# Batch 0's key maxima inside the convolution, and the last batch's first attention inside batch 0's key tile loop

## The reference, cut to what matters

```python
# layer 0: dynamic 31 tap mixing, 31 tap convolution 128 -> 512, selu, 512 -> 128
w = softmax(x @ Wl.T + bl);  y = sum_k w[..., k] * x[t + k]
z = selu(conv1d(y, Wc) + bc);  h = z @ W2.T + b2
# layer 0: causal self attention on layernorm(h), added to h, then a normalised copy added
h = h + softmax(mask(q k^T / 8)) v @ W_out + b_out;  h = h + layernorm(h)
# layer 1: cross attention of layernorm(h) on 7200 keys and values per batch
o = softmax((q w^T)(k w^T)^T / sqrt(128)) (v w^T) @ fc.T + residual;  then layernorm
# layer 1: 64 experts, top 6 of them, and shared experts
```

## Time and profile before

| | us |
|---|---|
| three runs: median (lowest to highest) | 1650.11 (1646.83 to 1660.38) |
| the profiled execution | 1647.7 |
| its span, first to last instruction | 1645.9 |
| PE busy | 1529.1 (93%) |
| DVE busy | 1052.4 (64%) |
| ACT busy | 721.6 (44%) |
| POOL busy | 559.5 (34%) |

### The profile page before, as it was taken

One profiled execution on the slowest core, in us unless ns is written; L12 is line 12 of the kernel. 1 busy time (PEld: TensorE's weight loads), 2 busy tenths in 40 slices (PEclk: granted clock), 3 DMA queues, 4 the chain that ended last, 5 costly groups with the idle time before them and its releaser, 6 DMA issues. The chain is left out here.

```text
span 1645.9 us, 30649 instructions
## 1 busy us (share of the span) xinstructions
PE 1529.1 (93%) x11598; PEld 1018.1 (62%) x11598; DVE 1052.4 (64%) x2087; ACT 721.6 (44%) x1269; POOL 559.5 (34%) x603
## 2 busy tenths in 40 slices
PE   2889998998997789999998999899999999999998
PEld 2556765765665447777777777678885444444444
DVE  4755545545234887776867777765565876877766
ACT  2231222222122126555554555456665665465554
POOL 2110001001004834602370235100795654555555
PEclk9999999999999879999999999999999999999999
DMA  8320100100001733602240223100122443344443
GB/s 218 89 89 23 29 26 17 29 26 21 1 1 53 184 88 78 143 1 73 59 123 21 65 72 94 37 23 2 54 85 88 131 130 92 123 136 132 138 130 107
DMA packets 142651, 124.74 MB, mean 76 GB/s; under 512 B 86613, under 2 KB 123949, under 8 KB 141485
## 3 DMA queue, kind: packets, MB, share of 16 engines
q1 hardware_dynamic: 127053, 110.62, 24.8%
q0 software_dynamic: 1152, 8.39, 1.6%
q10 hardware_dynamic: 14304, 3.81, 1.2%
HBM read 102.54 MB, written 5.28 MB: 66 GB/s over the span
## 5 line engine op out<-in xcount | busy, mean ns | idle before, releaser
L1186 DVE TENSOR_REDUCE region_c<-ps 120x1 f32<-120x512 f32 x336 | 225.6, 688 | 110.3 <-PE ps L1607 107.0
L873 ACT ACTIVATE region_c<-ps 128x720 f16<-128x720 f32 (+1 forms) x228 | 175.3, 769 | 274.5 <-PE ps L1637 274.5
L745 POOL TENSOR_TENSOR region_k<-region_c,region_k 128x480 f16<-128x480 f32 x198 | 217.1, 1100 | 174.0 <-ACT region_k L960 173.9
L1179 DVE TENSOR_TENSOR region_c<-ps,region_c 128x720 f16<-128x720 f32 (+1 forms) x228 | 206.1, 904 | 90.4 <-ACT ps L874 86.5
L1507 PE MATMUL ps<-region_k 128*128 128x360 f16 (+1 forms) x752 | 240.6, 320 | 5.2 <-ACT m L852 5.2
L1509 PE MATMUL ps<-region_k 128*128 128x360 f16 (+1 forms) x752 | 240.0, 319 | 0.0
L1508 PE MATMUL ps<-region_k 128*128 128x360 f16 (+1 forms) x752 | 239.7, 319 | 0.0
L665 POOL TENSOR_TENSOR vare<-mv,eps 120x6 f32<-120x6 f32 x20 | 4.0, 198 | 631.3 <-DVE mv L1111 631.3
L1654 PE MATMUL ps<-region_k,region_c 128*120 128x129 f16 (+1 forms) x1368 | 179.9, 221 | 0.0
L1655 PE MATMUL ps<-region_k,region_c 128*120 128x128 f16 (+1 forms) x1368 | 179.2, 220 | 0.0
L874 ACT ACTIVATE ps<-ps 128x720 f32<-128x720 f32 (+1 forms) x228 | 174.5, 766 | 0.0
(11 more groups left out here) (232 smaller groups left out, 2730.6 us busy)
## 6 DMA issues: line engine op xcount, KB each, us to landing
gates<-gates_dram SPq DMA_DIRECT2D x384, 120.0 KB, 2.8
region_c<-in_k SPq DMA_DIRECT2D x56, 256.0 KB, 2.7
region_c<-in_v SPq DMA_DIRECT2D x56, 256.0 KB, 2.9
region_c<-in_WcT POOLq DMA_DIRECT2D x8, 1024.0 KB, 6.4
region_c<-in_experts SPq DMA_DIRECT2D x18, 352.0 KB, 2.9
gates<-band_dram SPq DMA_DIRECT2D x26, 189.0 KB
region_k<-region_c SPq DMA_TRANSPOSE x120, 2.8
region_c<-in_xw SPq DMA_DIRECT2D x26, 63.0 KB
```

Source lines behind the costliest of these rows:

```text
L745: g.tensor_tensor(a_lo[u], ac[u], a_hi[u], ALU.subtract).then_inc(s["a_lo_ready"], 1)
L873: a.activation(halves(p_hi[u][0:parts]), st, ACT.Exp).then_inc(s["p_hi_ready"], 1)
L1179: v.tensor_tensor(halves(p_lo[u][0:parts]), two(2 * u, parts), halves(p_hi[u][0:parts]), ALU.subtract).then_inc(s["lo_ready"], 1)
L1186: v.tensor_reduce(mxk[:, r, bass.ds(c + 1, 1)], bank(bk, P), AX, ALU.max).then_inc(s["mx_free"], 1)
```

## The change

DVE's standalone list of batch 0's maxima (`prepare_tail(0)` to `shifts(0)`) goes as PE's does.

- Maxima of batch 0 become side steps of the convolution: 42 in batch 2 (quarters 6 to 47), 43 in batch 3 (quarters 0 to 42), each first in its quarter, in bank 3 with turns of `shared_turns`. Their keys come from a buffer `k16` (float16, one chunk), which GpSimd copies from `kf[0]`, whose load it issues itself (`stage_keys`); copies and variance powers are in one list on GpSimd. The maxima go to `mx0`, and `shifts(0)`, at quarter 44 of batch 3, writes `shift0`.
- The last batch's attention (`solo`) becomes steps beside batch 0's tiles 0 to 44, in bank 5 alone; on PE a step is one group: x 3 transposes, query one product of 360 columns, value 3 products of 128, score (and early) up to 480 columns, turn (and front) k + 1 transposes, weigh k + 1 products; scores of 5 and 6 blocks come in two parts (early, score; front, turn).  The end of that attention moves to tiles 45 to 56 and to tiles 0 to 14 of loop 1.
- Keys of batch 0 are split in its own loop, chunk by chunk in turn with batch 1's (`ITEMS`): chunks 0 and 1 of batch 0 before the convolution's end, then batch 1's n and batch 0's n + 2. SP's and GpSimd's lists follow it, without dynamic loops. PE waits per four tiles for batch 0's keys and turned values.
- After the convolution PE runs the first key scores, the down projections of the last batch, and goes on with the loop.

```diff
+def max_steps(b):
+    if b not in (B - 2, B - 1):
+        return []
+    if b == B - 2:
+        return [(6 + n, n) for n in range(R * NCH // 2)]
+    return [(n - R * NCH // 2, n) for n in range(R * NCH // 2, R * NCH + 1)]
...
+    steps += [(at, (MAX, 0, "max", n)) for at, n in max_steps(b)]
+    if b == B - 1:
+        steps.append((steps[-1][0] + 2, (MAX, 0, "shift", 0)))
...
-            if what not in ("logits", "band", "apply", "h"):
+            if what not in ("logits", "band", "apply", "h", "max"):
...
+END_STEPS = [("dve", "sum", 0, 0, 45), ("dve", "sum", 1, 0, 46), ("dve", "stats", 0, 0, 47), ("dve", "stats", 1, 0, 48),
+             ("dve", "stats", 2, 0, 49), ("act", "norm", 0, 0, 51), ("act", "norm", 1, 0, 52), ("dve", "add", 0, 0, 53),
+             ("dve", "add", 1, 0, 54), ("dve", "stats", 3, 0, 55), ("dve", "stats", 4, 0, 56),
+             ("dve", "stats", 5, 1, 0), ("act", "norm", 2, 1, 4), ("act", "norm", 3, 1, 5), ("pe", "x", 0, 1, 7),
+             ("act", "x", 0, 1, 8), ("pe", "x", 1, 1, 8), ("act", "x", 1, 1, 9), ("pe", "query", 0, 1, 9),
+             ("act", "query", 0, 1, 10), ("dve", "query", 0, 1, 11), ("pe", "query", 1, 1, 12),
+             ("act", "query", 1, 1, 13), ("dve", "query", 1, 1, 14)]
+SOLO_STEPS = ([("dve", "stats", 0, 0), ("dve", "stats", 1, 1), ("dve", "stats", 2, 1), ("act", "norm", 0, 4),
+               ("act", "norm", 1, 5)]
+              + [x for n, what in enumerate(("x", "query", "value")) for k in range(2)
+                 for x in (("pe", what, k, 5 + 2 * n + k), ("act", what, k, 6 + 2 * n + k))])
+for row, at in ((0, 11), (1, 16), (2, 21), (3, 26)):
+    SOLO_STEPS += [("pe", "score", row, at), ("dve", "score", row, at + 1), ("act", "score", row, at + 2),
+                   ("pe", "turn", row, at + 2), ("act", "turn", row, at + 3), ("pe", "weigh", row, at + 3),
+                   ("dve", "weigh", row, at + 4)]
+for row, at in ((4, 31), (5, 38)):
+    SOLO_STEPS += [("pe", "early", row, at), ("act", "early", row, at + 1), ("pe", "score", row, at + 1),
+                   ("dve", "score", row, at + 2), ("act", "score", row, at + 3), ("pe", "front", row, at + 3),
+                   ("act", "front", row, at + 4), ("pe", "turn", row, at + 4), ("act", "turn", row, at + 5),
+                   ("pe", "weigh", row, at + 5), ("dve", "weigh", row, at + 6)]
+SOLO, END, POST = "solo", "end", "post"
...
+ITEMS = [(0, "tail"), (0, 0), (0, 1), (1, "tail")]
+for n in range(NCH - 2):
+    ITEMS += [(1, n), (0, n + 2)]
+ITEMS += [(1, NCH - 2), (1, NCH - 1)] + [(b, c) for b in range(2, B) for c in ["tail"] + list(range(NCH))]
+DONE = {x: n + 1 for n, x in enumerate(ITEMS)}
+TURN = {x: n for n, x in enumerate(x for x in ITEMS if x[1] != "tail")}
...
+        k16 = region_c.take(CH, dtype=F16)
...
+            turns = list(TURN)
+            def turn_of(n):
+                b, c = turns[n]
+                if n == 0:
+                    sp.wait_ge(s["prod_full"], 3 * MC * B - 1)
+                if (b, c) == (1, 0):
+                    sp.wait_ge(s["shared_full"], len(SHARED))
+                turn(b, c)
+                if c == 0:
+                    turn_tail(b)
...
+                n = TURN[b, c]
+                u, at = n % 2, slice(c * CH, (c + 1) * CH)
+                if n >= 2:
+                    sp.wait_ge(s["klo_ready"], 2 + DONE[turns[n - 2]])
+                elif n == 0:
+                    sp.wait_ge(s["k16_ready"], NCH)
+                else:
+                    sp.wait_ge(s["shared_full"], SHARED[MAX, 0, "max", R * NCH][0])
+                sp.dma_start(kf[u], d["k"][b, :, at]).then_inc(s_kf[u], 16)
+                if n >= 2:
+                    sp.wait_ge(s["v_split"], DONE[turns[n - 2]])
+                sp.dma_start(vf[u], d["v"][b, :, at]).then_inc(s_vf[u], 16)
+                if n >= 2:
+                    turn_of(n - 2)
...
+            def stage_keys(c):
+                src, n = (kf[0], CH) if c < NCH else (kf_tail, TAIL)
+                if c < NCH:
+                    pool.wait_ge(s["k16_in"], 16 * (c + 1))
+                else:
+                    pool.wait_ge(s_tail, 32)
+                if c:
+                    pool.wait_ge(s["shared_full"], SHARED[MAX, 0, "max", R * c - 1][0])
+                g.tensor_copy(k16[:, 0:n], src).then_inc(s["k16_ready"], 1)
+                pool.wait_ge(s["k16_ready"], c + 1)
+                if c + 1 < NCH:
+                    pool.dma_start(kf[0], d["k"][0, :, (c + 1) * CH:(c + 2) * CH]).then_inc(s["k16_in"], 16)
+            pool.wait_ge(s["wprod_ps"], 1)
+            pool.dma_start(kf[0], d["k"][0, :, 0:CH]).then_inc(s["k16_in"], 16)
+            for b in range(1, B):
+                work = [(at + 0.25, "power", 3 * (b - 1) + x[3] + 1) for at, x in side_steps(b) if x[2] == "stats"]
+                work += [(at - 0.5, "keys", n // R) for at, n in max_steps(b) if n % R == 0]
+                for _, what, n in sorted(work):
+                    if what == "power":
+                        power_of_variance(n)
+                    else:
+                        stage_keys(n)
...
+            for b, c in ITEMS:
...
+            def first_maximum(n):
+                turn, bk = shared(0, "max", n, MAX)
+                dve.wait_ge(s["shared_full"], turn)
+                if n < R * NCH:
+                    own.link(v.tensor_reduce(mx0[:, n % R, n // R + 1:n // R + 2], bank(bk, P), AX, ALU.max))
+                else:
+                    own.link(v.tensor_reduce(mx0[:, :, 0], bank(bk, P)[:, 0:R * TAIL].rearrange("p (r k) -> p r k", r=R),
+                                             AX, ALU.max))
+                dve.sem_inc(s["dve_read"], 1)
...
+            def first_maximum(n):
+                if n == 0:
+                    pe.wait_ge(s["q_done"], 1)
+                pe.wait_ge(s["k16_ready"], n // R + 1)
+                _, bk, left, _ = SHARED[MAX, 0, "max", n]
+                pe.wait_ge(s[left[0]], left[1])
+                if n < R * NCH:
+                    last = mm(bank(bk, P), q_hi[:, 0, n % R * P:(n % R + 1) * P], k16, start=True, stop=True)
+                else:
+                    for r in range(R):
+                        last = mm(bank(bk, P)[:, r * TAIL:(r + 1) * TAIL], q_hi[:, 0, r * P:(r + 1) * P],
+                                  k16[:, 0:TAIL], start=True, stop=True)
+                last.then_inc(s["shared_full"], 1)
...
+            def solo(b, what, k):
+                x = h[:, b * R:(b + 1) * R, :]
+                if what == "stats":
+                    statistics(x, 3 * b + 1, (k,))
+                elif what == "score":
+                    dve.wait_ge(s["post_full"], USE[SOLO, b, what, k])
+                    n1 = (k + 1 if k < 4 else k - 2) * P
+                    diag = bank(5, P)[:, n1 - P:n1]
+                    own.link(v.tensor_tensor(diag, diag, causal[:], ALU.add))
+                    last = v.tensor_reduce(mx2[:, 0:1], bank(5, P)[:, 0:n1], AX, ALU.max)
+                    if k >= 4:
+                        dve.wait_ge(s["post_free"], USE[SOLO, b, "early", k])
+                        last = v.tensor_reduce(mx2[:, 1:2], pr_l[:, 0:HALF], AX, ALU.max)
+                    own.link(last)
+                    own.link(v.tensor_reduce(nm[:, k:k + 1], mx2[:, 0:1 + k // 4], AX, ALU.max, negate=True))
+                    dve.sem_inc(s["nmax_ready"], 1)
+                else:
+                    dve.wait_ge(s["post_full"], USE[SOLO, b, what, k])
+                    own.link(v.tensor_reduce(den[:, k:k + 1], sums[:, k, 0:1 + k // 4], AX, ALU.add))
+                    own.link(v.reciprocal(rden[:, k:k + 1], den[:, k:k + 1]))
+                    own.link(v.scalar_tensor_tensor(out=x[:, k, :], in0=bank(5, P)[:, 0:C], scalar=rden[:, k:k + 1],
+                                                    in1=x[:, k, :], op0=ALU.mult, op1=ALU.add))
+                    dve.sem_inc(s["post_free"], 1)
...
+                if b == 0 and t % 4 == 0:
+                    pe.wait_ge(s["klo_ready"], 2 + DONE[b, t // 4 if t < KT else "tail"])
+                at = slice(t * KW, t * KW + parts)
...
-            prepare_tail(0)
-            for k in range(2):
-                down(B - 1, k)
-            for c in range(NCH):
-                for u in range(2):
-                    for r in range(3 * u, 3 * u + 3):
-                        maximum_of(0, c // 2, c % 2, r)
-                    for what, k in LAST_ATTN_STEPS[2 * c + u:2 * c + u + 1]:
-                        attn(B - 1, what, k)
-            pe.wait_ge(s["mx_free"], MAXIMA + 1)
             pe.wait_ge(s["q_done"], B - 1)
             for b in range(B):
-                pe.wait_ge(s["klo_ready"], 2 + CHUNKS * (b + 1))
-                for u in range(2):
-                    pe.wait_ge(s_vt[u], 32 * (NCH // 2) * (b + 1))
-                pe.wait_ge(s_vt_tail, 32 * (b + 1))
-                pe.wait_ge(s["ones_columns"], b + 1 if b < 2 else 2)
+                if b:
```

(56 more changed lines are left out.)

238 lines of the change are left out of this document (132 added, 106 removed).

## The result

The changed kernel takes 1691.84 us (median of four runs, 1686.4 to 1695.31) against 1649.53 for the kernel before (four runs, 1646.83 to 1660.38). The ratio is 1.0247, 95% interval 1.022 to 1.0274. 1673 was forecast with a range of 1628 to 1694; the forecast's own range ended at 1690. The profiled execution of the changed kernel took 1686.4 us, the fastest of its four; its span is 1684.6, that of before was 1645.9. These 38.7 us are divided up here (the medians differ by 42.3).

A forecast was written before the change was run, and what follows sets the result against it. In-order TensorE, busy 95 to 99% in convolution batches 2 and 3 and the tile loops, was taken as the bound. 1647.7 - 78 (stage) + 84 (convolution) + 17 + 3 (loops) = 1673.7, say 1673 us; range 1628 to 1694.

The forecast's parts named there:

- The stage removed: Between convolution and tile loop: batch 0's maxima stage goes, saving 76.2 us, and about 2 more from starting at full clock.
- TensorE time of the maxima: Convolution batches 2 and 3: the maxima's 512 columns take 0.21 us each on TensorE, 18 us.
- (a): Convolution: band, apply or h steps wait until VectorE has reduced the maximum in bank 3; 25 us, from 10 to 32.
- (b): Convolution, ends of products 1 and 2: maxima wait behind VectorE's eviction and selu; 13 us, from 6 to 18.
- (c): Convolution: maxima wait for GpSimd's key copies queued behind variance powers, two gaps of 7.1 us included; 27 us, from 12 to 32.
- old waits: Convolution: today's TensorE waits belong to the same chains and are covered by the new ones; -7 us.
- (d): Convolution: gaps without matmuls bring three half clock spells; 8 us, from 3 to 20.
- Loop 0: Batch 0's tile loop: the attention adds TensorE work and waits for low parts; +17 us, from +12 to +24.
- the fourth rival: Loop 0: GpSimd paces it at 5.7 us a chunk, costing 5 us or so, 1678 us; chance 0.03.
- the other two that rested on overlap: Convolution: bank 3 waits overlap, not add; 1630 us (chance 0.20), or with half that overlap 1650, no change (0.20).
- Loop 1: Batch 1's tile loop: the end of the attention in its first 15 tiles; +3 us, from +2 to +8.
- The third rival: Convolution: the clock stays low through most of batches 2 and 3, 8 spells not three; +20, 1693 us; chance 0.12.

The follow-up runs named there:

- The last experiment: The version with quarter 36, with GpSimd also waiting for the convolution's last selu before splitting batch 1's key tail: 1646.62 us, lowest of versions that compute everything.
- the second kind of maxima: Changed kernel with 16 batch 2 maxima left out whose quarters have no band or apply step: 1688.48 us, ratio 1.0223.
- The experiment with GpSimd's order: Changed kernel with GpSimd's key copies put ahead of the variance powers, the powers one quarter later: 1666.75 us, ratio 1.0109.
- the version with quarter 36: Changed kernel with maxima in mid-quarter, key copies ahead of variance powers, and quarters 8, 20 and 36 free of maxima: 1650.66 us, ratio 1.001.

## Why the prediction was right or wrong, point by point

- **The stage removed, -76.2 and -2.** 73.3 was measured. The loop proper starts 13.0 us behind the convolution and not 10.2. The step said that the down projections "stay"; the first took 4.31 us in place of 2.88 and started 4.2 us after the end in place of 2.7. The cause is the selu held up by GpSimd and the half clock that followed. The wait in front of the down projection was not longer than before, 2.25 us against 2.33, and the earlier one stayed at full clock. The last experiment takes both away. The loop itself starts at full clock, as forecast: the product of 360 columns at its beginning has 0.47 us.
- **TensorE time of the maxima, 18.** Not seen alone. The 0.2 us of the second kind of maxima is no check of it: it is fewer waits and columns less more half clock.
- **(a) 25, (b) 13, (c) 27, old waits -7.** Measured 22.7, 13.5 and 24.8, with 6.6 of old waits gone. In all 54.7 us of idle time against 58. The places are right too: eight band and eight apply waits, the two gaps of 7.1 us at quarter 35 (7.18 both). The single waits of (b) do not follow from its own figures (4.0 and 3.6 less 2.04 are 2.0 and 1.6, not 2.1 and 1.3). And the terms are less independent than the sum takes them to be: with GpSimd's waits gone, 9 us came back as waits of maxima for VectorE.
- **(d) Clock, 8.** This is the term that was mis-sized. "The two waits of 7 us will do the same, and I take one or two of the shorter clusters: three spells": there were eight, 37.4 us, for 15 to 19 us. Only two of them, the long ones, lie at the 7 us gaps; the other six begin within 1.4 us of the end of gaps of 2.3 to 3.7 us, one of them behind two of 1.2 and 1.3 close together. Before, with 7.8 us of idle time in two batches and 2.7 the longest wait, the clock had stayed at 1.00. The experiment with GpSimd's order bears it out: it gave back 13 us of waits and 9 of busy time.
- **Loop 0, +17, and 168 us from the tail maxima on.** 168.8. The attention's own cost by experiment is 20.1 (16.5 busy, 3.6 waits) against 19. GpSimd's split of both batches is hidden, so the fourth rival is refuted, and the other two that rested on overlap (1630 and 1650) with it: VectorE's idle half of batch 2 did not make the sum of the waits smaller than forecast.
- **Loop 1, +3.** +5.0; the waits for the low parts went from 5.7 us to 6.8.
- **The third rival** ("8 spells and not three", 1693) is what happened, in the count and in the time (1691.8). It had got 0.12, on the ground that batch 2 had three waits of up to 2.7 us at full clock. Three waits were no evidence for what thirty do. That its time is so near is partly luck: in the profiled executions only 7 to 11 of the 12.7 us above the forecast can be the clock, where it had asked for 20. Its picture of a clock that stays low through most of the batches is not what happened: between the spells the clock is full.

In the profiled executions the forecast's sum was +26.0 and the change +38.7. The difference of 12.7 is 9.9 in the convolution (busy time 13.2 above the 18 + 8 forecast, idle time 3.3 below the 58), 2.9 at the loop's start, 2.0 in loop 1, 1.3 in loop 0, and some -3 outside the change.

Undone where it hurt, the change still gains nothing. The columns (18 us) were the smaller part of its price. Of the 61 us of waits, 22.7 are steps that wait for the bank that a maximum borrowed, 13.5 maxima that wait for VectorE and 24.8 maxima that wait for GpSimd's copy, all on an in-order TensorE that was busy for 96% of batch 2. In the best version TensorE's idle time in the convolution is still 23 us above the kernel before, and its busy time 32.

## What to carry to other kernels

Before work is moved from a stage with slack into one where an in-order engine is nearly full, count the buffers it shares there: a step in a quarter without another user of its bank cost 0.2 us, the same step in front of one about 1.9, and 2.3 with the gap of a late copy. When many short waits come in, price the clock as well: moving GpSimd's work took 13 us of waits away and gave 9 back in busy time, moving the maxima 14 and 3. And look at what a helper engine does in the few microseconds in which everyone waits for one chain: starting it 3 us later gave 3.7 us, 1.7 of them half clock.

## What the runs showed of the hardware

**VectorE's operations from SBUF to SBUF wait for GpSimd's.** Alone, the three TENSOR_SCALAR operations on 128 x 360 float32 take 0.41, 0.40 and 0.35 us and the two-input one 0.53. Beside GpSimd's split they took 0.72, 0.74, 1.20 and 0.82 in the changed kernel, and up to 1.39 in the version above. It doesn't look like sharing: in the timelines of the version with quarter 36 each of the four VectorE operations ends 0.2 to 0.4 us after the GpSimd instruction that was under way when it started (576.25 after 576.05; 577.49 after 577.28; 578.16 after 577.96; 579.58 after 579.19), and in the changed kernel it is the same for the last three (612.95 after 612.75; 614.19 after 613.98; 615.05 after 614.66). GpSimd lost less: its casts of 512 columns took 0.68 to 0.93 us beside them and 0.61 otherwise. VectorE operations that read PSUM with two inputs kept their duration (the 720 column low part has 0.90 us in loop 0, whether GpSimd is busy for 30% of it as before or for 52%). The Trainium skill (SBUF — State Buffer, SBUF: two separate sides) describes an exclusive lock, which goes for a whole instruction to whichever starts first, a GpSimd operation or a VectorE operation that is in a two-port mode or, against a GpSimd operation that reads SBUF, has two SBUF inputs. The end times agree with it; which mode VectorE's operations were in no trace shows. The prediction had priced this only as a slower GpSimd in loop 0, where it did no harm, and not as a slower VectorE on the one chain that was exposed.

**The clock.** Half clock spells came behind two gaps of 7.18 us, and also at gaps of 2.3 to 3.7 us. The length of the gap alone does not tell: the kernel before had waits of 2.7 and 2.33 us at full clock (the second at the end of the convolution), while in the kernel without the 84 maxima a wait of 2.8 us, with none above 1 us before it in its batch, had a spell of 3.4 us behind it. The 7 us gaps were followed by spells of 10.2 and 6.8 us, the others by 3.4 each. In the kernel without the 84 maxima batch 2 ran at 1.00.
